# Splitting the last 64 filter-tap products of a convolution/attention kernel around the first attention products

## The reference, cut to what matters

```
x = x + silu(batchnorm(hypergraph_conv(group_norm(x))))      # L0
t = tokens(x)                                                # (4, 256, 32)
t = t + attn(layer_norm(t))        # softmax(z z^T) z, z = layer_norm(t)
t = t + stu(layer_norm(t))         # sum over 16 filters of causal convolutions along
                                   # tokens, with 32x32 mixing matrices and 3 direct taps
x = from_tokens(t)
```

## Time and profile before

| | us |
|---|---|
| median of 3 runs (lowest to highest) | 52.59 (52.2 to 52.71) |
| the profiled execution's own time | 52.18 |
| its span, from first to last instruction | 50.4 |
| TensorE busy | 42.9 (85%) |
| VectorE / ScalarE / GpSimd busy | 23.3 / 21.0 / 9.6 |
| mean granted TensorE clock | 0.999 |

### The profile page before, as it was taken

How to read it: one execution, slowest core, us unless ns; L and a number is a source line. 1 busy time by engine, 2 the same in 40 slices (tenths; PEclk the granted TensorE clock), 3 DMA queues, 4 the chain that set the end, 5 groups by cost and what they waited for, 6 DMA issues and landing times.

```text
span 50.4 us, 1575 instructions
## 1 busy us (share of the span) xinstructions
PE 42.9 (85%) x658; PEld 25.5 (51%) x658; DVE 23.3 (46%) x81; ACT 21.0 (42%) x55; POOL 9.6 (19%) x36
## 2 busy tenths in 40 slices
PE   2999994999879999787999968648999999999910
PEld 1332743564436974436787424226455646548800
DVE  1057629999756460326648775745001400403420
ACT  0664999805222992499895882050003100000000
POOL 4760408880002275000000000430000000000000
PEclk9999999999999999999999999999999999999999
DMA  0599400000000000000000000000000000000011
GB/s 0 145 311 362 142 0 0 0 0 0 13 0 0 0 20 0 0 0 0 0 13 0 0 13 0 0 0 0 0 0 0 7 0 0 13 0 0 0 52 52
DMA packets 1303, 1.44 MB, mean 29 GB/s; under 512 B 272, under 2 KB 1040, under 8 KB 1296
## 3 DMA queue, kind: packets, MB, share of 16 engines
q1 hardware_dynamic: 1008, 1.26, 7.8%
q10 hardware_dynamic: 288, 0.08, 0.7%
HBM read 1.21 MB, written 0.13 MB: 27 GB/s over the span
## 4 chain that ended last, share of the span: by engine, by line
PE 57%; DVE 13%; ACT 9%; issue 7%; POOL 5%; DMA 4%; POOLq 0%; DVEq 0%
PE bank L536 22%; PE bank L362 8%; DMA x_sb<-in_x 4%; PE bank L579 4%; PE bank L350 3%; PE bank L370 3%; PE quad L527 3%; ACT L252 3%; PE bank L478 2%; PE quad L492 2%; PE bank L503 2%; DVE hgraph L647 2%; POOL h L202 1%; PE quad L469 1%; POOL tiny L205 1%
## 5 line engine op out<-in xcount | busy, mean ns | idle before, releaser
L536 PE MATMUL bank<-v,gh 128*128 128x512 f16 (+7 forms) x48 | 7.5, 317 | 0.0
L536 PEld LDWEIGHTS bank<-v,gh 128*128 128x128 f16 x48 | 4.2, 98 | 3.4 <-issue 0.2
L252 ACT ACT_TABLE_LOAD x4 | 5.1, 1283 | 1.7 <-PEq L852 1.6
L337 PE MATMUL bank<-busy 128*128 128x512 f16 x9 | 4.0, 629 | 0.9 <-DVE busy L613 0.9
L536 PE MATMUL bank<-v,gl 128*128 128x512 f16 (+7 forms) x24 | 3.8, 317 | 0.8 <-DVE v L775 0.8
L362 PE MATMUL bank<-phis,mst 32*32 32x64 f32 x256 | 4.2, 289 | 0.0
L788 DVE TENSOR_TENSOR yb<-bank,maskp 128x512 f32<-128x512 f32 x2 | 1.4, 690 | 5.9 <-PE bank L536 5.9
L362 PEld LDWEIGHTS bank<-phis,mst 32*32 32x32 f32 x256 | 3.7, 110 | 0.5 <-issue 0.5
L647 DVE TENSOR_SCALAR hgraph<-quad,thr 128x256 f16<-128x256 f32 x8 | 3.4, 471 | 0.4 <-PE quad L392 0.4
L337 PE MATMUL quad<-busy 128*128 128x512 f16 x10 | 3.3, 381 | 0.0
L536 PEld LDWEIGHTS bank<-v,gl 128*128 128x128 f16 x24 | 2.0, 98 | 2.4 <-issue 1.1
(11 more groups left out here) (171 smaller groups left out, 77.3 us busy)
## 6 DMA issues: line engine op xcount, KB each, us to landing
m_sb<-in_mfilt SPq DMA_DIRECT2D x1, 512.0 KB, 3.6
cst<-in_consts SPq DMA_DIRECT2D x1, 271.0 KB, 3.8
x_sb<-in_x SPq DMA_DIRECT2D x1, 128.0 KB, 2.1
phi_sb<-in_phi SPq DMA_DIRECT2D x1, 128.0 KB, 2.5
out<-res SPq DMA_DIRECT2D x2, 64.0 KB, 1.5
sml<-in_small ACTq DMA_DIRECT2D x1, 64.0 KB, 2.6
mu_sb<-in_mu SPq DMA_DIRECT2D x1, 64.0 KB, 3.5
sml<-in_small ACTq DMA_DIRECT2D x1, 12.0 KB, 2.3
```

The source lines that it names most:

```text
L252: act.activation(spare[:, len(loads) - 1:len(loads)], eps[:, 0:1], func)
L337: pe.matmul(dst, busy[:, 0:1].broadcast_to([P, P]), busy[:, 0:1].broadcast_to([P, 512]), start=True, stop=True)
L536: mm = pe.matmul(acc[:, :, lag:HT], g[:, s, :, :].rearrange("p e a -> p (e a)"), v2[:, part, :, begin + lag:begin + HT], start=(first and ...
```

## The change

The helper `taps` gets a first and a last step, and the call for row groups 2 and 3 is cut in two: steps 0 to 5 stay where they were, and steps 6 and 7 (16 matmuls, 32 records, with the signals) are issued after the four AV matmuls of the first half of the keys. The count of instructions, the data and all other engines' lists stay as they are.

```diff
-            def taps(pair):
-
-                for e in range(EG):
+            def taps(pair, first=0, last=EG):
+
+                for e in range(first, last):
                     for n in pair:
                         r = slice(32 * n, 32 * n + 32)
                         for q in range(PH):
...
             pe.wait_ge(sem("g_low0"), 1)
-            taps((2, 3))
+            taps((2, 3), 0, 6)
 
             pe.wait_ge(sem("zt"), 1)
             for n in range(2):
...
                 if n == 0:
+                    taps((2, 3), 6, EG)
                     pe.wait_ge(sem("g_low1"), 1)
                     pe.wait_ge(sem("rden"), 1)
                     turn_rows(gbank[1], rden[:, :, :].rearrange("p h b -> p (h b)"), "rden_psum0", (0,))
```

## The result

The changed kernel takes 52.67 us (median of 22 runs, 52.49 to 53.21) against 52.64 us (22 runs, 52.08 to 53.65). The ratio of the two is 1.0061, 95% interval 1.0033 to 1.0089: slower by 0.6%, or 0.17 to 0.47 us, which is clear of no change and less than 1%. The two medians hide it, since the runs of each kernel fall in two clusters some 0.5 us apart, and the ratio hides part of it too: of the kernel before, 14 runs are in its upper cluster and 6 in its lower one (two more took over 53.5 us), of the changed one 10 and 12. Cluster against cluster, the changed kernel is 0.44 us slower in the lower one (mean 52.59 against 52.14) and 0.43 in the upper one (53.09 against 52.66). Its span is 50.8 us against 50.4, the granted clock 1.0 against 0.999.

A forecast was written before the change was run, and what follows sets the result against it. TensorE, busy 85% of the span, was taken to bound the stage up to AV's last matmul. Terms -0.06 + 0.27 + 0 = +0.21 us gave 52.39 on the profile, 52.8 us on the median, range 52.3 to 53.2.

The forecast's parts named there:

- the +0.21 of the sum: Whole kernel: -0.06 + 0.27 + 0 = +0.21 us, 52.18 to 52.39 on the profiled execution, 52.8 on the median.
- the forecast's own +0.1 to +0.35: Whole kernel: the band of loss in us that the prediction named as its forecast, chance 0.60.
- Two added changes of tile shape, +0.27: TensorE between AV's first half and the first spread: taps to 128 by 32 costs 0.16, the way back 0.11 us.
- The rival that each change costs as the widest hole: TensorE between AV's first half and first spread: 2 x 0.33 - 0.06 = +0.60 us, 53.2 median; chance 0.10.
- The 175 ns by which the prediction priced a drain: TensorE at the two switches: a drain of about 175 ns each would make 0.35 instead of 0.27 us.
- The exponential's wait, -0.06: AV's second half on TensorE: the last matmul's 0.06 us wait for exponential 8 goes if that half starts later.
- `g_high(2)` later by 0.73: VectorE: the cast starts later by AV's first half and both changes before it, 0.46 + 0.16 + 0.11 us.
- VectorE: Term 0: VectorE behind the later signal g_psum2: slack takes up the 0.73 us delay, so it adds 0 us.
- the step that gave 0.45 us of slack at the square: Second layer normalization: centring product's result there at 29.24, square held by ScalarE's table load to 29.69, hence 0.45 us slack.
- The other step, 0.26 idle ahead of `wo`: VectorE ahead of `wo`: 0.26 us idle taken as slack, so `wo` moves by only 0.47 of the 0.73 us.
- VectorE's queue becomes the bound: VectorE's queue: decides if `g_high(2)` starts over 0.9 us later (0.45 + 0.21 + 0.26), giving 53.0 us; chance 0.12.
- The signs to look for: Changed trace: AV earlier, two holes, cast near 27.36, `o_sb` near 28.1, no idle ahead of `wo`, square released by ScalarE.

The follow-up runs named there:

- e1: Kernel before with a single tap matmul (two records) moved behind AV's first half, the late signal g_psum2 left out: ratio 1.0087.
- e4: Changed kernel with the second portion of taps cut again, step 6 ahead of the first spread and step 7 behind it: ratio 1.0185 to the kernel before.
- e11: Changed kernel with seven steps of taps ahead of AV's first half and one (16 records) behind it: 52.59 us in a single run.
- e5: e3 with AV's end signalled once, by the last of its four matmuls, instead of by each: ratio 1.0054 to the kernel before.
- e2: Kernel before with a VectorE product of 640 float32 columns put ahead of g_high(2), about 0.7 us of delay, TensorE's list untouched: ratio 1.0085.
- e3: Changed kernel with VectorE's list reordered: both reciprocals first, then g_high(2), wo, and g_low(2) only behind wo: ratio 1.0087 to the kernel before.
- e7: Kernel before with the copy o_sb on VectorE, the square-root table loaded after the last exponential, and g_low(2), t2, g_high(3) moved: ratio 0.9958.
- e6: Kernel before without the two dummy matmuls ahead of the first layer normalization's centring product (line 472): ratio 0.9933.
- e10: e6 and e7 together with one signal for AV's end, plus one dummy matmul between the second layer normalization's centring products: ratio 0.9877 to the kernel before, 51.68 us.

## Why the prediction was right in sign, and where it was not

The forecast of a loss below 1% came true, and 52.67 us lies near the 52.8 forecast. The second is partly luck. Like compared with like, the loss is +0.40 in the trace and +0.43 to +0.44 between clusters, twice the +0.21 of the sum and outside the forecast's own +0.1 to +0.35; the median comes out close because fewer runs of the changed kernel fell in the upper cluster. One term was right, one small term failed, and the term that was put at 0 decided the outcome.

- **Two added changes of tile shape, +0.27: right.** Measured 0.11 (AV to taps, 0.57 for 0.46) + 0.15 (0.60 for 0.45) + 0.02 at the spread = 0.28. e1 and e4 show that it comes with the changes of shape, e11 that it does not follow the portion's size down to 16 records; a portion of two costs more, 0.43 at the start of AV's second half (e1). The rival that each change costs as the widest hole is out: the hole ahead of the second portion is 0.41 us wide, twice what I expected and wider than any of the earlier trace rows, and AV's first half occupies only 0.11 more for it. The 175 ns by which the prediction priced a drain stand on the page of the Trainium skill, "TensorE: Matmul & The Clock Gate", section Single matmul latency, as the constant part of one lone bf16 matmul's time; as the price of a change they would make 0.35, and the measured 0.28 decides.
- **The exponential's wait, -0.06: failed.** The wait went (it was 0.09, 0.61 covered instead of 0.70) and `o_sb` gained nothing; the four signals took its place (e5).
- **`g_high(2)` later by 0.73: right to the hundredth.**
- **"VectorE: Term 0": failed, at the step that gave 0.45 us of slack at the square.** The chain's piece of 0.45 for line 472 was read as the length of a centring product. It is the slice of the product that is left behind the dummies' end (18.92 + 0.60 = 19.52). The whole product covers 0.59, with its weights loaded under running matmuls, and one from a standing start, that is, one whose weight load also waits for the operand, 0.70 (line 516 before, 517 after). With 0.70, and 0.04 and not 0.02 from its end to the square, the slack is 29.69 - (28.78 + 0.70 + 0.04) = 0.17. The other step, 0.26 idle ahead of `wo`, was 0.08 too generous. Slack 0.36 in all (e2) against a delay of 0.73 makes +0.37 at the square; measured 0.39, and 0.38 in e2 without any added change of shape. In e4 the same sum gives 0.87 for 0.88.
- **The sum.** +0.21 was forecast; the trace has +0.40 and the ratio +0.32 (0.17 to 0.47). The rival "VectorE's queue becomes the bound", given a chance of 0.12, is what happened; its 53.0 is +0.41 on the 52.59 of then. Its threshold, a cast over 0.9 us late, was the wrong part of it: about 0.6 was enough (0.36 + 0.27). It cost only 0.13 beyond TensorE's share of 0.27 (e3), since delays side by side don't add.
- **The signs to look for.** AV's first record at S + 3.04, the two holes (0.41 and 0.21), the cast at 27.42 and no idle ahead of `wo` all came; `o_sb` stood at 28.23, and the square was released by TensorE, which I had named as what would make me wrong.

Open: why `wo` starts 0.08 us after `g_low(2)` when it is next in the queue and its other operands are there; it waits on three semaphores, and no run took one away. In e7 the same three waits stand between the copy and `wo`, and `wo` starts 0.03 after the copy's end (28.92, then 28.95), so they don't cost 0.08 by themselves.

## What to carry to other kernels

Interleaving small matmuls on a saturated engine was free here only between products of one tile shape; count the changes of shape before and after, and price each by the spacing of starts. Where a measured time falls in clusters, compare cluster with cluster before believing a median or a ratio. A slice of the chain of waits is no duration: take an operation's length from a place where it starts under the same conditions, and compare the two ends that meet at a wait rather than the one the chain prints. Where an end-of-work signal moves, follow the other engine's queue behind it with its real slack.

## What the runs showed of the hardware

- A change from 128 by 32 to 32 by 32 tiles and back costs about 0.27 us of TensorE with 16 or more records between (e11, changed, e4), and 0.43 with a single matmul (e1), whose 0.32 us is the least a lone portion occupied. The hole that the weight loads show ahead of the portion, 0.41 us, is no measure of that cost.
- Four matmuls that end together with a signal each delay the waiting engine by 0.15 us after the last modelled end (changed kernel); one signal by 0.07 (e5).
- A float32 product of 128 by 256 takes 0.70 us from a standing start and 0.59 queued behind running matmuls with its operands ready (line 472 before, behind dummies, and in e6, behind line 469). A dummy ahead of its wait did not bring that back (e10).
